# A selective scan on one core: products, scans and B's broadcast share four PSUM banks, and each group's product moves ahead of the last scan before it

## The chip, the core and the metric

The kernel runs on one core of a Trainium2 chip. The metric is device time in microseconds, the median of several executions. Engines are named as in the profile: PE (matmuls, with PEld for its weight loads), DVE (VectorE), ACT (ScalarE), POOL (GpSimd) and SP, which only issues DMAs here. Each engine runs its own list of instructions in order; engines meet at semaphores.

## The reference, cut to what matters

The input is x, 16 samples of 64 x 64 positions x 96 channels. Layer 0 normalises x, resamples it, runs a small two-layer network and adds the result to x. Layer 1 normalises again and runs a Mamba block over the 4096 positions of each sample. Its core, per channel d (192 of them) and state n (16 of them), is

```python
dA  = exp(delta[..., None] * A)
dBu = delta[..., None] * Bm[:, :, None, :] * xc[..., None]
def step(h, inp):                # one position after the other
    dA_t, dBu_t, C_t = inp
    h = dA_t * h + dBu_t
    y = einsum('bdn,bn->bd', h, C_t)
    return (h, y)
```

and its output is gated, projected and added to the layer's input.

## The kernel before

A sample is cut into 8 chunks of T = 512 positions. In a chunk there are 192 x 16 pairs (d, n) = 24 tiles of 128 partitions x 512 positions. A tile is a unit n = 0..23; three units are a group g = 0..7 of the chunk, so a sample has 64 groups and the kernel 1024. A unit needs: on ACT the exponential `av` (L1008, eight buffers); on DVE the scan `hs` (L1140, `tensor_tensor_scan`, six buffers), which reads `av` from SBUF and its row of products from PSUM; on POOL the product with C, `hc` (L1181, six buffers), and after the group's third unit a copy of the last column, `state` (L1185). PE sums over n into `py` (L855, function `reduce`), after the group's three `hc`.

The products themselves are made once per group. PE spreads B's row over the partitions into the PSUM bank `pb` (L846, `spread_b`, one bf16 matmul), and DVE multiplies `rep_u` (delta times x, from SBUF) by `pb` into the three banks of `b3` (L1134, one instruction of 128 x 1536). In the order of DVE's list a group is: product, scan 0, scan 1, scan 2. The product waits for the broadcast (`pe_b`) and for the scan before it (`dve_h`, since it overwrites what that scan reads); scan 0 waits for the product (`dve_bu`) and for the `state` of two groups before (`pool_st`); each scan waits for its `av`. PE's broadcast for group g waits until the product of group g-1 is done, and stands in PE's list after unit 3g-2, before the `reduce` of group g-2 (after unit 3g-1).

PE, ACT and DVE have a second stream of work between the units: layer 0 of the samples ahead and the projections of the chunks ahead. Its steps are rows (position, step) of a plan, where a position is a unit of the sample, 0 to 191. PE works a row off after the unit of its position; ACT evicts it 4 units later (`LAG`), DVE does its part 3 units later. The results take turns in three PSUM banks `cb`, each freed by its eviction. The plan's function `level` spreads PE's steps by assumed costs, and `warm` fills the lightly loaded groups with dummy matmuls (L710). The steps that matter below, all in groups 32 to 35 of a sample: `DG` at position 98 makes a bias, and DVE adds a constant to it into `cst` (L1123) after unit 101; `D_lo`, `D_hi` from position 100 on (PE L794, L798), whose evictions on ACT (L965) wait for `cst`; `WG` at 102, evicted by DVE into `b1a` (L1120), for which the first `W_f` (PE L769) waits; `X` at 104 and 106 (PE L810), evicted by ACT with a silu (L982). From there to about group 29 of the next sample the second stream is dense. The plan of the last sample but one has less of it, and that of the last has only the projections and the output step `OUT` (PE L837, L838). One product of the stream, the padding step at the end of a plan, is evicted by DVE (L1100).

Of the kernel before, what the change touches and what calls it, by code (L numbers as in the profile page):

```python
# [9 lines left out]
ALU = mybir.AluOpType  # L10
ACT = mybir.ActivationFunctionType

NS, HH, WW, C = 16, 64, 64, 96
# [8 lines left out]
T = 512  # L22
NC8 = L // T
NJ, NQ = DI // 32, DSTATE // 4
NU = NJ * NQ
NG = NU // 3
NHC, NAV, NHS = 6, 8, 6
# [170 lines left out]
def build(nc, A):  # L198
    ctx = ExitStack()
    with ctx:  # L200
        def sb(name, shape, dt=F32):
            return ctx.enter_context(nc.sbuf_tensor(name, shape, dt))

        def ps(name, shape):
            return ctx.enter_context(nc.psum_tensor(name, shape, F32))
# [37 lines left out]
        selb = sb("selb", [C, NQ, 128], BF16)  # L243
# [39 lines left out]
        bc3 = sb("bc3", [C, 4, T], BF16)  # L283
        rep_d = sb("rep_d", [128, 2, NJ, T])
        rep_u = sb("rep_u", [128, 2, NJ, T])
        cs = sb("cs", [128, 2, NQ, T])
        av = sb("av", [128, NAV, T])
        hs = sb("hs", [128, NHS, T])
# [10 lines left out]
        yv = sb("yv", [C, T])  # L299

        cb = ps("cb", [128, RING, 512])
        b3 = ps("b3", [128, 3, 512])
        pb = ps("pb", [128, 512])
        py = ps("py", [128, 512])

        ld_s = sem("ld_s")
# [36 lines left out]
        ru_ld = [sem("ru_ld0"), sem("ru_ld1")]  # L343
        cs_ld = [sem("cs_ld0"), sem("cs_ld1")]
        pe_b = sem("pe_b")
        act_a = sem("act_a")
        dve_bu = sem("dve_bu")
        dve_h = sem("dve_h")
# [8 lines left out]

        xtok = A["x"].rearrange("s h w c -> s (h w) c")
        otok = A["out"].rearrange("s h w c -> s (h w) c")

        def rows_of(m):

# [120 lines left out]
        def count(sm, v):  # L483

            return max(v, 0)
# [8 lines left out]
        def _(sp):  # L494
# [136 lines left out]
            def c_part(st, k, n):  # L631
                G = st.s * NC8 + k
                at = AT["sp"]
                if not ((G < -1 or G + 1 >= NS * NC8)):

                    p = (k + 1) % 2
                    if n == at["du"]:
                        sp.wait_ge(pool_u, count(pool_u, G + 2))
                        sp.sem_inc(sp_passed, 1)
                        sp.dma_start(du_d[p].rearrange("(t p) f -> p t f", p=C), dlt[:, :, :]).then_inc(du_st, 16)  # L640
                    if n == at["rd"][0]:
                        sp.wait_ge(dl_st, count(dl_st, (G + 2) * 16))
                        sp.sem_inc(sp_passed, 1)
                        sp.wait_ge(act_a, count(act_a, G * NU))
                        sp.sem_inc(sp_passed, 1)
# [43 lines left out]
        def _(pe):  # L689
# [151 lines left out]
            def spread_b(G, k, g):  # L841

                if g == 0:
                    pe.wait_ge(pool_bc, count(pool_bc, G * 2 + 2))
                pe.wait_ge(dve_bu, count(dve_bu, G * NG + g))
                pe.matmul(pb[:, :], selb[:, g % NQ, :], bc3[:, k % 4, :], start=True, stop=True).then_inc(pe_b, 1)  # L846

            def reduce(s, k, g):
                G = s * NC8 + k
# [205 lines left out]
        @block.vector  # L1055
        def _(dve):
            dve.memset(wx[:, :, :], 0.0).then_inc(zset, 1)
            dve.memset(bc3[:, :, :], 0.0).then_inc(zset, 1)
            dve.memset(mhalf[:, :], -0.5)
            dve.memset(eps[:, :], 1e-5)  # L1060
            dve.memset(zero_state[:, :], 0.0)
            dve.memset(zero2[:, :], 0.0).then_inc(zset, 1)
            dve.wait_ge(ld_w, count(ld_w, 16 * len(loads)))
            n_set = [0]

            def setup(ins):
                n_set[0] += 1
                ins.then_inc(setup_v, 1)
                dve.wait_ge(setup_v, count(setup_v, n_set[0]))

            for f in range(NF):
                setup(dve.tensor_scalar(g2[:, 1, f, 0:C], w2t[:, f, :], coef[:, f, 1:2], None, ALU.mult))
            setup(dve.tensor_tensor(fcst[:, :], b1t[:, :], coef[:, :, 1], ALU.mult))
            setup(dve.tensor_tensor(fcst[:, :], fcst[:, :], coef[:, :, 0], ALU.add))
            for f in range(NF):
                setup(dve.tensor_scalar(w2c[:, f, :], w2t[:, f, :], coef[:, f, 2:3], None, ALU.mult))

            for tap in range(3):
                setup(dve.tensor_tensor(wtap[:, tap, :, :], winx.rearrange("c (t p) -> c t p", t=2),
                                        cwb.rearrange("c (p t k) -> c k t p", t=2, k=3)[:, tap], ALU.mult))  # L1080

            def finish():
                dve.wait_ge(setup_a, count(setup_a, 2))
                setup(dve.tensor_scalar(nega[:, :, :], nega[:, :, :], -1.0, None, ALU.mult))
                dve.wait_ge(pe_conv, count(pe_conv, N_FIRST + 3))
                dve.tensor_copy(wlin[:, :], cb[0:C, 0, 0:C]).then_inc(cb_free[0], 1)
                dve.tensor_tensor(cbase[:, :], cb[0:C, 1, 0:1], b2t[:, :], ALU.add).then_inc(cb_free[1], 1)
                dve.tensor_copy(spare[:, 2:3], cb[0:C, 2, 0:1]).then_inc(cb_free[2], 1)
                assert n_set[0] == N_SETUP

            def step(st, key):
                name, b = key[:2]
                if name in ("SLD", "WLD", "DLD", "DW", "WARM", "SG1", "SG2", "DG1", "DG2") or name in BATCHED or name == "OUT":
                    return
                i = st.at[key]
                bank = cb[:, i % RING]
                fr = cb_free[i % RING]
                if name == "PAD":
                    dve.wait_ge(pe_conv, st.done(i))
                    dve.tensor_copy(spare[:, i % RING:i % RING + 1], bank[0:C, 0:1]).then_inc(fr, 1)  # L1100
                    return
                x = st.sample(key)
                if name == "ST":
                    dve.wait_ge(fr, st.freed(i))
                    dve.bn_stats(bst[:, 0, b, :], xs_of(b)).then_inc(xs_bn, 1)
                    if b == 7:
                        dve.wait_ge(xs_bn, count(xs_bn, x * 8 + 8))
                        dve.wait_ge(act_v[0], count(act_v[0], x))
                        dve.bn_aggr(mv[:, 0, :], bst[:, 0].rearrange("c a b -> c (a b)")).then_inc(dve_m[0], 1)
                elif name == "D_hi":  # L1110
                    for bank_free, n_free in st.freed_all([i, st.find(("D_lo", b), key)]):
                        dve.wait_ge(bank_free, n_free)
                    dve.bn_stats(bst[:, 1, b, :], x1s[:, b % 2, :]).then_inc(x1_bn, 1)
                    if b == 7:
                        dve.wait_ge(x1_bn, count(x1_bn, x * 8 + 8))
                        dve.wait_ge(act_v[1], count(act_v[1], x))
                        dve.bn_aggr(mv[:, 1, :], bst[:, 1].rearrange("c a b -> c (a b)")).then_inc(dve_m[1], 1)
                elif name == "WG":
                    dve.wait_ge(pe_conv, st.done(i))
                    dve.tensor_tensor(b1a[:, :], bank[:, 0:NF], b1t[:, :], ALU.add).then_inc(fr, 1)  # L1120
                elif name == "DG":
                    dve.wait_ge(pe_conv, st.done(i))
                    dve.tensor_tensor(cst[:, :], bank[0:C, 0:1], cbase[:, :], ALU.add).then_inc(fr, 1)  # L1123

            def unit(s, k, n):
                G = s * NC8 + k
                hf, g, q = n // 12, n // 3, n // 3 % NQ
                if n == 0:
                    dve.wait_ge(ru_ld[k % 2], count(ru_ld[k % 2], s * (4 * 64) + (k // 2 + 1) * 64))
                if n % 3 == 0:  # L1130

                    dve.wait_ge(pe_b, count(pe_b, G * NG + g + 1))
                    dve.wait_ge(dve_h, count(dve_h, G * NU + n))  # L1133
                    dve.tensor_tensor(b3[:, :, :], rep_u[:, k % 2, 3 * hf:3 * hf + 3, :],  # L1134
                                      pb[:, None, :].broadcast_to([128, 3, T]), ALU.mult).then_inc(dve_bu, 1)
                    dve.wait_ge(pool_st, count(pool_st, G * NG + g + 1 - NHS // 3))
                    dve.wait_ge(dve_bu, count(dve_bu, G * NG + g + 1))
                dve.wait_ge(act_a, count(act_a, G * NU + n + 1))  # L1138
                start = state[:, g, n % 3:n % 3 + 1] if k > 0 else zero_state[:, 0:1]
                dve.tensor_tensor_scan(hs[:, n % NHS, :], av[:, n % NAV, :], b3[:, n % 3, :], start, ALU.mult, ALU.add)\  # L1140
                    .then_inc(dve_h, 1)

            run(lambda row: row[0] + LAG["bn" if row[1][0] in ("ST", "D_hi") else "dve"], unit, step, lambda st, k, n: None, lambda st, k, n: None, finish)

        @block.gpsimd
# [158 lines left out]
```

## Time and profile before

| what | value |
|---|---|
| runs: median (lowest to highest) of 3 | 6343.9 us (6341.24 to 6345.12) |
| profiled execution, first to last instruction | 6343.7 us, 99100 instructions |
| busy: PE, DVE, ACT, POOL | 95%, 90%, 80%, 82% of the span |
| scans L1140 | 3072, mean 1263 and 1264 ns |
| products L1134 | 1024, mean 1761 ns |
| broadcasts L846 | 1024, mean 397 ns |
| first and last product start | 328.2 and 6322.1 us |

The profiled execution's own time is its span, 6343.7 us; it lies 0.2 us below the median of the runs. Busy shares are averages over the whole span; PE's matmuls are pipelined, so a busy PE is not PE at its peak. A full sample lasts about 375.6 us; the sixth one, from 2216.1 to 2591.7 us, is taken below as the example.

### The profile page before, as it was taken

What the parts mean: (1) busy time and instruction counts of PE and PEld (TensorE: products, weight loads), DVE (VectorE), ACT (ScalarE), POOL (GpSimd) and SP (SyncE); (2) the same over time, 40 slices, a digit from 0 to 9 for tenths busy, and PEclk for the clock granted to TensorE, in tenths of its full rate; (3) what the DMA queues carried; (4) which work ended last, traced back from release to release, by engine and by line L of the source; (5) the groups of instructions that cost most, each with busy time, mean ns of one, the idle gap of its engine ahead of it and who ended that gap; (6) DMA issues with size and microseconds to landing.
All of it is one profiled execution on the core that took longest, in us unless ns stands there. A gap on an engine that the chain in (4) does not pass through costs nothing. (4 is left out here: it accounts for less than half of the span.)

```text
span 6343.7 us, 99100 instructions
## 1 busy us (share of the span) xinstructions
PE 6036.5 (95%) x32260; PEld 3123.0 (49%) x32260; DVE 5685.5 (90%) x4459; ACT 5097.3 (80%) x8658; POOL 5209.8 (82%) x5092
## 2 busy tenths in 40 slices
PE   8999999999999999999999999999999999998776
PEld 5645445454554545545455544545455454554222
DVE  0089999999999999999999999999999999999998
ACT  4588888888888888888888788888888888887664
POOL 0078888888888888888888888888888888888988
PEclk9999999999999999999999999999999999998665
DMA  3367676676767667675676767667676766767553
GB/s 95 88 165 170 160 167 157 163 162 169 169 154 168 155 165 170 155 182 142 167 162 162 173 156 169 155 164 163 167 169 156 166 154 165 168 142 160 129 124 75
DMA packets 805826, 983.25 MB, mean 155 GB/s; under 512 B 391258, under 2 KB 417542, under 8 KB 805318
## 3 DMA queue, kind: packets, MB, share of 16 engines
q1 hardware_dynamic: 805318, 976.92, 65.4%
q8 instruction: 265, 4.34, 0.3%
q14 instruction: 243, 1.99, 0.1%
HBM read 717.71 MB, written 259.00 MB: 154 GB/s over the span
## 5 line engine op out<-in xcount | busy, mean ns | idle before, releaser
L1181 POOL TENSOR_TENSOR hc<-hs,cs 128x512 f32<-128x512 f32 x3072 | 3835.6, 1271 | 692.7 <-DVE hs L1140 505.6
L1140 DVE TENSOR_TENSOR_SCAN hs<-av,state,b 128x512 f32<-128x512 f32 x2688 | 3257.8, 1263 | 88.6 <-POOL state L1185 4.9
L1008 ACT ACTIVATE av<-rep_d,nega 128x512 f32<-128x512 f32 x3072 | 2096.7, 713 | 41.5 <-DVE hs L1140 36.8
L1134 DVE TENSOR_TENSOR b<-rep_u,pb 128x1536 f32<-128x1536 f32 x1024 | 1803.5, 1761 | 211.0 <-PE pb L846 124.7
L855 PE MATMUL py<-hc,rsel 128*32 128x512 f32 x6144 | 1141.6, 634 | 40.6 <-POOL hc L1181 39.7
L769 PE MATMUL cb<-xu,w1a 96*128 96x392 f32 x2400 | 984.3, 513 | 27.7 <-DVE b1a L1120 17.4
L774 PEld LDWEIGHTS cb<-w2c,g 128*98 128x98 f32 x9600 | 885.9, 167 | 169.7 <-issue 106.9
L774 PE MATMUL cb<-w2c,g 128*98 128x96 f32 x9600 | 910.7, 252 | 17.4 <-ACT g L956 9.3
L956 ACT ACTIVATE g<-cb,b1a 128x392 f32<-128x392 f32 x1200 | 679.5, 579 | 87.0 <-PE cb L769 78.8
L810 PE MATMUL cb<-xn,wtap 96*96 96x512 f32 x1536 | 723.3, 607 | 2.4 <-ACT xn L1029 2.4
L769 PEld LDWEIGHTS cb<-xu,w1a 96*128 96x128 f32 x2400 | 414.5, 191 | 415.4 <-issue 199.3
L846 PE MATMUL pb<-bc,selb 96*128 96x512 bf16 x1024 | 406.6, 397 | 140.5 <-DVE b L1134 140.4
L1140 DVE TENSOR_TENSOR_SCAN hs<-av,zero_state,b 128x512 f32<-128x512 f32 x384 | 466.9, 1264 | 11.8
L949 ACT ACTIVATE vr<-cb 98x384 f32<-98x384 f32 x400 | 194.9, 487 | 320.2 <-PE cb L774 318.2
L810 PEld LDWEIGHTS cb<-xn,wtap 96*96 96x96 f32 x1536 | 243.5, 166 | 400.4 <-issue 380.0
L855 PEld LDWEIGHTS py<-hc,rsel 128*32 128x32 f32 x6144 | 157.2, 110 | 455.7 <-POOL hc L1181 225.0
L1218 POOL TENSOR_TENSOR dlt<-dlt,xcs 96x1024 f32<-96x1024 f32 x128 | 301.8, 2358 | 68.5 <-DMA delta_scratch<-dlt 68.5
L846 PEld LDWEIGHTS pb<-bc,selb 96*128 96x128 bf16 x1024 | 103.7, 101 | 508.1 <-issue 246.3
L763 PE MATMUL cb<-up_h,t1r 128*96 128x196 f32 x1600 | 345.7, 339 | 7.7 <-DMA t1r<-t_scratch 7.5
L837 PE MATMUL cb<-wo,xcs 96*128 96x96 f32 x2048 | 341.0, 292 | 3.7 <-POOL xcs L1233 3.5
L1233 POOL TENSOR_TENSOR xcs<-xcs,zs 96x512 f32<-96x512 f32 x256 | 324.1, 1266 | 20.1
L837 PEld LDWEIGHTS cb<-wo,xcs 96*128 96x128 f32 x2048 | 291.5, 205 | 86.0 <-issue 49.5
(109 smaller groups left out, 6703.4 us busy)
## 6 DMA issues: line engine op xcount, KB each, us to landing
rep_d<-delta_scratch SPq DMA_DIRECT2D x512, 384.0 KB, 7.0
rep_u<-deltax_scratch SPq DMA_DIRECT2D x512, 384.0 KB, 6.3
cs<-c_scratch SPq DMA_DIRECT2D x512, 256.0 KB, 5.9
delta_scratch<-dlt SPq DMA_DIRECT2D x128, 384.0 KB, 3.1
deltax_scratch<-dlt SPq DMA_DIRECT2D x128, 384.0 KB, 9.2
t1r<-t_scratch SPq DMA_DIRECT2D x160, 240.0 KB, 6.5
v_scratch<-v2s SPq DMA_DIRECT2D x192, 192.0 KB
xb<-in_x SPq DMA_DIRECT2D x128, 192.0 KB, 4.6
```

The costliest lines, as they stand in the source:

```text
L763: mm = pe.matmul(bank[0:C, e * 2 * GH:(e + 1) * 2 * GH], t1r[:, m % 2, i2 % 5, :], up_h[:, :], start=True, stop=True)
L769: mm = pe.matmul(bank[:, 0:BC], w1a[:, 128 * f:128 * f + 128], xu[:, b % 2, :], start=True, stop=True)
L774: mm = pe.matmul(bank[0:GH, C * j:C * j + C], g2[:, b % 2, f, GH * j:GH * j + GH], w2c[:, f, :], start=(f == 0), stop=(f == NF - 1))
L810: mm = pe.matmul(bank[0:C, :], wtap[:, tap, t, :], xn[:, k2 % 2, tap:tap + T], start=(tap == 0), stop=(tap == 2))
L837: pe.matmul(o, xcs[:, p, t, tb], wo[:, t, :], start=(t == 0), stop=False)
L846: pe.matmul(pb[:, :], selb[:, g % NQ, :], bc3[:, k % 4, :], start=True, stop=True).then_inc(pe_b, 1)
L855: mm = pe.matmul(py[32 * j:32 * j + 32, :], rsel[:, :], hc[:, (3 * g + j) % NHC, :], start=(q == 0), stop=(q == NQ - 1), skip_group_check= ...
L956: act.activation(g2[:, b % 2, f, :], bank[:, 0:BC], ACT.Square, bias=b1a[:, f:f + 1]).then_inc(fr, 1)
L1008: act.activation(av[:, n % NAV, :], rep_d[:, k % 2, j, :], ACT.Exp, scale=nega[:, q, j:j + 1])\
L1134: dve.tensor_tensor(b3[:, :, :], rep_u[:, k % 2, 3 * hf:3 * hf + 3, :], pb[:, None, :].broadcast_to([128, 3, T]), ALU.mult).then_inc(dve_b ...
L1140: dve.tensor_tensor_scan(hs[:, n % NHS, :], av[:, n % NAV, :], b3[:, n % 3, :], start, ALU.mult, ALU.add)\
L1181: pool.tensor_tensor(hc[:, n % NHC, :], hs[:, n % NHS, :], cs[:, k % 2, g % NQ, :], ALU.mult)\
```

## The change

The banks `b3` and `pb` become one tensor of four banks, `b4`. Group by group the three product banks are 2, 1, 0 (even groups, walked backwards) or 1, 2, 3 (odd groups), and the broadcast is put into the bank of the group's third product, 0 or 3; the product instruction overwrites it in place. The two banks of the first two products of a group are those that the group before has already scanned, so the product needs only that group's first two scans. In DVE's list the order becomes: scan 0, scan 1, product of the next group, scan 2. PE's broadcast for group g waits for the scans of group g-2 in place of the product of group g-1, as its bank is that of group g-2's third product.

```diff
-        b3 = ps("b3", [128, 3, 512])
-        pb = ps("pb", [128, 512])
+        b4 = ps("b4", [128, 4, 512])
...
+        def banks(g):
+            return b4[:, 2::-1, :] if g % 2 == 0 else b4[:, 1:4, :]
+        def bank_of(g, e):
+            return 2 - e if g % 2 == 0 else 1 + e
...
-                pe.wait_ge(dve_bu, count(dve_bu, G * NG + g))
-                pe.matmul(pb[:, :], selb[:, g % NQ, :], bc3[:, k % 4, :], start=True, stop=True).then_inc(pe_b, 1)
+                pe.wait_ge(dve_h, count(dve_h, (G * NG + g - 1) * 3))
+                pe.matmul(b4[:, bank_of(g, 2), :], selb[:, g % NQ, :], bc3[:, k % 4, :], start=True, stop=True)\
+                    .then_inc(pe_b, 1)
...
+            def times_b(G, g):
+                k = G % NC8
+                if g == 0:
+                    dve.wait_ge(ru_ld[k % 2], count(ru_ld[k % 2], G // NC8 * (4 * 64) + (k // 2 + 1) * 64))
+                dve.wait_ge(pe_b, count(pe_b, G * NG + g + 1))
+                dve.wait_ge(dve_h, count(dve_h, (G * NG + g) * 3 - 1))
+                out, hf = banks(g), g // NQ
+                b = b4[:, bank_of(g, 2), :]
+                dve.tensor_tensor(out, rep_u[:, k % 2, 3 * hf:3 * hf + 3, :], b[:, None, :].broadcast_to([128, 3, T]), ALU.mult)\
+                    .then_inc(dve_bu, 1)
+
             def unit(s, k, n):
...
+                if G == 0 and n == 0:
+                    times_b(0, 0)
                 if n % 3 == 0:
-
-                    dve.wait_ge(pe_b, count(pe_b, G * NG + g + 1))
-                    dve.wait_ge(dve_h, count(dve_h, G * NU + n))
-                    dve.tensor_tensor(b3[:, :, :], rep_u[:, k % 2, 3 * hf:3 * hf + 3, :],
-                                      pb[:, None, :].broadcast_to([128, 3, T]), ALU.mult).then_inc(dve_bu, 1)
                     dve.wait_ge(pool_st, count(pool_st, G * NG + g + 1 - NHS // 3))
                     dve.wait_ge(dve_bu, count(dve_bu, G * NG + g + 1))
+                if n % 3 == 2 and not (G + 1 == NS * NC8 and g + 1 == NG):
+                    times_b(G + (g + 1) // NG, (g + 1) % NG)
                 dve.wait_ge(act_a, count(act_a, G * NU + n + 1))
```

The wait for `rep_u` at a chunk's first product moves with the product. Nothing else in the plan, the lags or the other engines' lists is changed.

## Rows read from the trace of the kernel before

**Rows 1.** Windows view: the sixth sample and the last two; columns named at the top.

```profile
core 0: us, PE busy (x) PEld busy (x) DVE busy (x) ACT busy (x) POOL busy (x), PEclk, DMA share, GB/s
...
2216.10:2591.70 375.60, 368.81 (x2024) 192.05 (x2021) 354.71 (x278) 317.15 (x542) 325.61 (x319) 1.00 0.69 163
...
5606.00:5970.30 364.30, 311.12 (x1457) 145.65 (x1451) 349.50 (x268) 273.00 (x442) 323.04 (x316) 0.85 0.64 145
5970.30:6322.10 351.80, 247.87 (x769) 79.21 (x764) 339.27 (x253) 214.68 (x322) 312.20 (x305) 0.63 0.49 111
```

**Rows 2.** Waits of DVE over five full samples: total us, times, longest.

```profile
DVE b L1134 <- PE pb L846: 37.7, 56, 1.3
```

**Rows 3.** Waits of PE in the sixth sample that DVE or POOL ended.

```profile
PE cb L769 <- DVE b1a L1120: 1.3, 1, 1.3
PE py L855 <- POOL hc L1181: 1.1, 3, 0.4
PE cb L794 <- DVE cst L1123: 0.8, 1, 0.8
PE pb L846 <- DVE b L1134: 0.7, 2, 0.4
```

**Rows 4.** Timeline of DVE, groups 26 to 35: start us, us, work, [idle before].

```profile
2368.83 1.76 DVE L1134 TENSOR_TENSOR b<-rep_u,pb 128x1536 f32<-128x1536 f32 x1 [0.99 <-PE pb L846]
...
2386.81 1.76 DVE L1134 TENSOR_TENSOR b<-rep_u,pb 128x1536 f32<-128x1536 f32 x1
2388.66 3.62 DVE L1140 TENSOR_TENSOR_SCAN hs<-av,state,b 128x512 f32<-128x512 f32 x3
2392.39 1.76 DVE L1134 TENSOR_TENSOR b<-rep_u,pb 128x1536 f32<-128x1536 f32 x1
...
2411.01 3.63 DVE L1140 TENSOR_TENSOR_SCAN hs<-av,state,b 128x512 f32<-128x512 f32 x3
2414.56 0.12 DVE L1123 TENSOR_TENSOR cst<-cb,cbase 96x1 f32<-96x1 f32 x1
...
2423.38 0.66 DVE L1113 BATCH_NORM_STATS2 bst<-x1s 96x6 f32<-96x512 f32 x1
2423.96 0.14 DVE L1120 TENSOR_TENSOR b1a<-cb,b1t 128x3 f32<-128x3 f32 x1
```

**Rows 5.** Timeline of PE in the same stretch.

```profile
2368.41 0.38 PE L846 MATMUL pb<-bc,selb 96*128 96x512 bf16 x1
...
2386.08 0.38 PE L846 MATMUL pb<-bc,selb 96*128 96x512 bf16 x1
...
2414.74 0.67 PE L794 MATMUL cb<-xt,wtot 96*96 96x256 f32 x2 [0.77 <-DVE cst L1123]
...
2425.17 2.82 PE L810 MATMUL cb<-xn,wtap 96*96 96x512 f32 x6
```

**Rows 6.** Timeline of ACT in the same stretch.

```profile
2409.26 1.32 ACT L1008 ACTIVATE av<-rep_d,nega 128x512 f32<-128x512 f32 x2
2414.77 0.47 ACT L965 ACTIVATE x1s<-cb,cst 96x256 f32<-96x256 f32 x1 [4.18 <-issue]
...
2424.43 0.68 ACT L982 ACTIVATE xcs<-cb,tapb 96x512 f32<-96x512 f32 x1
```

**Rows 7.** Timeline of POOL in the same stretch.

```profile
2390.09 3.73 POOL L1181 TENSOR_TENSOR hc<-hs,cs 128x512 f32<-128x512 f32 x3 [1.73 <-DVE hs L1140]
...
2409.14 3.71 POOL L1181 TENSOR_TENSOR hc<-hs,cs 128x512 f32<-128x512 f32 x3
```

**Rows 8.** Timeline of PE in the last sample, around one output step.

```profile
6005.64 0.61 PE L846 MATMUL pb<-bc,selb 96*128 96x512 bf16 x1 [2.05 <-DVE b L1134]
6006.18 1.93 PE L855 MATMUL py<-hc,rsel 128*32 128x512 f32 x6
...
6013.27 0.63 PE L846 MATMUL pb<-bc,selb 96*128 96x512 bf16 x1
```

**Rows 9.** Timeline of DVE at the same place.

```profile
6003.82 1.76 DVE L1134 TENSOR_TENSOR b<-rep_u,pb 128x1536 f32<-128x1536 f32 x1
```

**Rows 10.** Windows view of the same place; columns as in the first group.

```profile
6003.00:6026.00 23.00, 15.56 (x54) 6.31 (x52) 22.19 (x17) 15.84 (x25) 22.61 (x22) 0.50 0.50 123
```

More of the change, by code:

```diff
@@ L1123, in step @@
                     dve.tensor_tensor(cst[:, :], bank[0:C, 0:1], cbase[:, :], ALU.add).then_inc(fr, 1)
+            def times_b(G, g):
[8 more added lines that the diff above has]
+                    .then_inc(dve_bu, 1)
             def unit(s, k, n):
[L1126 to L1129, printed above, removed]
+                G, g = s * NC8 + k, n // 3
+                if G == 0 and n == 0:
+                    times_b(0, 0)
                 if n % 3 == 0:
-                    dve.wait_ge(pe_b, count(pe_b, G * NG + g + 1))
-                    dve.wait_ge(dve_h, count(dve_h, G * NU + n))
-                    dve.tensor_tensor(b3[:, :, :], rep_u[:, k % 2, 3 * hf:3 * hf + 3, :],
-                                      pb[:, None, :].broadcast_to([128, 3, T]), ALU.mult).then_inc(dve_bu, 1)
                     dve.wait_ge(pool_st, count(pool_st, G * NG + g + 1 - NHS // 3))
                     dve.wait_ge(dve_bu, count(dve_bu, G * NG + g + 1))
+                if n % 3 == 2 and not (G + 1 == NS * NC8 and g + 1 == NG):
+                    times_b(G + (g + 1) // NG, (g + 1) % NG)
                 dve.wait_ge(act_a, count(act_a, G * NU + n + 1))
                 start = state[:, g, n % 3:n % 3 + 1] if k > 0 else zero_state[:, 0:1]
-                dve.tensor_tensor_scan(hs[:, n % NHS, :], av[:, n % NAV, :], b3[:, n % 3, :], start, ALU.mult, ALU.add)\
-                    .then_inc(dve_h, 1)
+                dve.tensor_tensor_scan(hs[:, n % NHS, :], av[:, n % NAV, :], b4[:, bank_of(g, n % 3), :], start,
+                                       ALU.mult, ALU.add).then_inc(dve_h, 1)
             run(lambda row: row[0] + LAG["bn" if row[1][0] in ("ST", "D_hi") else "dve"], unit, step, lambda st, k, n: None, lambda st, k, n: None, finish)
```

## Prediction

> **What bounds the kernel now.** I read the windows by sample first. Fourteen of the sixteen samples carry the dense second stream; one lasts 375.6 us, and PE is busy in 368.8 and DVE in 354.7 of them [rows 1]. Shares so close together do not say which engine leads, so the next view is who waits for whom. DVE waits for PE's broadcast 37.7 us in five samples, 7.5 us a sample [rows 2]. PE waits for DVE or POOL only 1.3 + 1.1 + 0.8 + 0.7 = 3.9 us a sample [rows 3]; 0.7 of that, two of 64 broadcasts, is the wait that the change loosens. The reader should see the asymmetry: most of the time PE goes at its own pace (with ACT, which empties its banks) and DVE follows.
>
> The timeline shows where. At 2368.83 the product begins 0.04 us after its broadcast (2368.41 + 0.38), having waited 0.99 us: PE leads there [rows 4, 5]. At 2386.81 the product of group 29 starts without a wait, 0.35 us after its broadcast (2386.08 + 0.38), and from there to 2414.74 DVE runs without one. At 2414.74 PE waits 0.77 us for `cst`, and ACT, which had nothing to issue past that eviction, stood still for 4.18 us [rows 5, 6]. So DVE's chain sets the pace in one short stretch of a sample, groups 29 to 35, and PE with ACT in the rest. In the last sample PE's granted clock is 0.63 on average and its busy time 247.9 of 351.8 us [rows 1]: there DVE leads.
>
> **The change, part by part.** *DVE's cycle.* Now a product takes 1.76, scan 0 follows 0.09 after its end, three scans take 3.62, and the next product starts 0.11 later (2388.66 + 3.62 to 2392.39): 5.58 us a group [rows 4]. The two gaps are waits for DVE's own results. Where no such wait stands, an instruction starts before its predecessor is recorded as ended: the statistics at 2423.38 end at 2424.04, the next instruction starts at 2423.96, 0.08 earlier [rows 4]. Three scans in 3.62 with two such overlaps make one scan 1.26. In the new order only the product waits for the scan just before it. Product to scan 2 is 1.76 - 0.08 = 1.68, scan 2 to scan 0 and scan 0 to scan 1 are 1.18 each, scan 1 takes 1.26, then the gap of 0.11: 5.41, so 0.17 less. Bounds: 0, if a scan does not overlap the product ahead of it, to 0.20 if all three junctions and the gap come out a little better. I take 0.17, the row's own overlap.
>
> A rule of the Trainium skill speaks against that saving. "VectorE: DVE Perf Modes", section "The DRAIN you can't avoid", states that the next DVE instruction does not start until the pipeline of the last has emptied, and that taking semaphores away saves nothing. The 0.08 overlap above disagrees with it. By the rule the cycle stays at 5.58; the time is then that of rival C.
>
> *In place, and the reversed banks.* No row has DVE reading and writing one PSUM bank. In-place cost bounds: nothing below; above, if reading and writing that third of the product took turns, 512 of 1536 columns twice, 1.76 / 3 = 0.59 us a group. I take nothing: the four-bank form moves as many elements, and one engine goes over them in one order. The backward walk over banks has the same bounds.
>
> *PE's broadcast.* Its release moves from the end of product g-1 to the end of group g-2's third scan. Counted from the start of product g-1, that was 1.76 + 0.06 (6003.82 to 6005.64 [rows 8, 9]) and becomes 1.68 + 1.26 + 0.06 = 3.0, since that scan now follows the product. Product g starts 5.41 after product g-1, so with 0.38 for the matmul 2.0 us of slack remain, before 3.4. Instructions behind it on PE (a `reduce`, then steps) are held with it only where PE is early.
>
> *DVE's place relative to PE.* This is the price. Where a product is released by its broadcast, the group's scans used to follow at once. Now scan 2 of the group before comes first: relative to the same broadcast everything DVE does comes later, scans 0 and 1 by 1.0 us (1.68 + 1.18 against 1.85), and what stands behind a third scan by far more, as the next group's product is put ahead of it. `cst` is such a step: it stands after unit 101, the third scan of group 33, and so now also behind the product of group 34.
>
> *The stretch from group 29, walked through.* The broadcast of group 29 ends at 2386.46 either way (2386.08 + 0.38), as PE leads up to it. DVE, one scan later relative to PE, now just waits for it: product at 2386.50 instead of 2386.81. Five cycles of 5.41 and 0.03 for the chunk's boundary put the product of group 34 at 2413.58 (now 2414.74). Its scan 2, of group 33, starts 1.68 later at 2415.26, and `cst` 1.18 after that at 2416.44, ending 2416.56. Now it ends at 2414.68 [rows 4]. It comes 1.9 us later.
>
> ACT then starts its queue at 2416.65 instead of 2414.77. From there it works without a pause to the silu of the first `X`, 2424.43 to 2425.11, and PE's second `X` at 2425.17 waits for just that bank [rows 5, 6]. It moves to 2427.1. POOL does not change this: its `hc` of group 29 waits for DVE [rows 7], its last one ends about 2.4 us later than now, and POOL is then busy without a gap to 2412.85, which becomes 2415.2; PE's `reduce` of group 32 then ends at about 2416.1, ahead of `cst`. `b1a` comes 0.6 later by the same count, at 2424.7, and is hidden by the 2427.1. From here PE leads again, now 1.9 us late, and DVE's shorter cycle only makes it wait longer: 11 us a sample (64 x 0.17).
>
> *Other edges*, at nothing: the `rep_u` wait moves one scan up, but by the code its loads are issued after units 7 to 13 of the chunk before, which leaves more than three groups; `pool_st` has a cycle of 5.4 us, and DVE has slack where POOL is late. If those covers were gone, DVE would wait at a chunk's first product or first scan.
>
> **The sum.** Fourteen stretches x 1.9 = +26.6 us. The last two samples: 128 cycles x 0.17 = -21.8. Against it, at a granted clock of 0.50, the 1.2 GHz level (PE was idle for a third of this sample), the broadcast after an output step comes late: it was 7.63 us after the one before it (6005.64 to 6013.27 [rows 8, 10]). From the product at 6003.82 the count is now 2.94 to the third scan's end, 1.45 until POOL's `hc` lets the `reduce` start (a third of 3.73 for the multiply [rows 7], and the waits), 7.09 from it to the broadcast and 0.63 for it: 12.1, while the product could start after two cycles, 10.85. That is 1.3 us in each of about ten chunks, +13. For some five other places in the sample before the last where the broadcast is already close, I add one scan each, 1.2 us, an estimate: +6. Together -3. The forecast is 6343.7 + 26.6 - 3 = 6367 us; the span is 0.2 below the median of the runs, so the same number stands for the median: 0.37% slower.
>
> **Rivals.** *A, faster.* DVE leads everywhere, and each group saves 0.17: 1024 x 0.17 = 174, 6170 us. For it: the chain of waits ends in DVE's rows, and DVE's cycle repeats at 5.58. Against it: 7.5 us a sample of waiting for broadcasts. A milder form is bounded by PE's own waits, 3.9 us a sample: if `cst` came no later than now, the loosened broadcast let PE run ahead and ACT did not bind, 14 x 3.9 = 55 less, 6289. It decides at `cst`: before 2414.7 on the clock above, faster; after, slower. Chance 0.16 for both, mostly values a little under 6331.
>
> *B, no change.* The second eviction of `D` and ACT's queue catch up: ACT stood still for 4.18 us there with its exponentials several units ahead of DVE, and if the wait of `X` had room of 1.9 us that the row does not show, the +26.6 falls away and -3 is left: 6341. Chance 0.20.
>
> *C, slower by more.* No saving in the cycle: then `cst` ends at 2386.50 + 5 x 5.58 + 0.03 + 1.85 + 1.18 + 0.13 = 2417.7, 3.0 late, +42, and the last two samples lose about 10 (ten chunks x 0.95 and little else): 6396. Or the product in place costs up to 0.59: DVE's own time, 368 a sample (375.6 - 7.5), grows by 64 x (0.59 - 0.17) = 27 to 395, 16 x 19 = +310, 6654. From +0.3 us a product it passes PE's pace. Chance 0.08 for both.
>
> **How the numbers follow.** The forecast has 0.56. Within 0.2%, about 13 us and what a measurement of this kernel can tell from no change, lies B. Slower holds the forecast and C, 0.64; faster A, 0.16; same 0.20. The likeliest case alone, with the saving between 0.20 and 0.10, ranges from 6358 to 6380. The range takes in B and the first half of C and leaves A's far end and the in-place price out: 6328 to 6394.
>
> **What would show it.** Right: products of about 1.76 us and unwaited cycles of 5.41; DVE's waits for broadcasts grown from 7.5 to some 20 us a sample; a sample of 377.5 us; ACT's idle time before L965 grown from 4.2 to about 6 us, and PE's wait for `cst` from 0.8 to over 2. Wrong: a sample shorter than 375 us, products longer than 1.8 us, cycles still at 5.58, or PE waiting for broadcasts.

## The result and the profile after

The changed kernel takes 6435.0 us against 6342.8 us (medians of four runs each); the ratio of the means is 1.0142, 95% interval 1.0128 to 1.0157. The forecast was 6367 us, slower by 0.37%; the sign was right and the loss is four times as large, outside the range. The profiled execution's span is 6436.1 us, 92.4 more than before. The page's costliest groups that the change touches, the product with C and the product with B on the page of before and then all three after:

```profile
L1181 POOL TENSOR_TENSOR hc<-hs,cs 128x512 f32<-128x512 f32 x3072 | 3835.6, 1271 | 692.7 <-DVE hs L1140 505.6
L1134 DVE TENSOR_TENSOR b<-rep_u,pb 128x1536 f32<-128x1536 f32 x1024 | 1803.5, 1761 | 211.0 <-PE pb L846 124.7
```
```profile
L1197 POOL TENSOR_TENSOR hc<-hs,cs 128x512 f32<-128x512 f32 x3072 | 3855.1, 1273 | 814.6 <-DVE hs L1156 766.7
L1156 DVE TENSOR_TENSOR_SCAN hs<-av,state,b 128x512 f32<-128x512 f32 x2688 | 3255.4, 1261 | 0.4 <-POOL state L1201 0.4
L1142 DVE TENSOR_TENSOR b<-rep_u,b 128x1536 f32<-128x1536 f32 x1024 | 1804.3, 1762 | 533.3 <-PE b L853 480.5
```

Product and scans last what they did. What grew is waiting: DVE's for the broadcast (124.7 to 480.5 us), POOL's for the scans (505.6 to 766.7 us). The windows view of the sixth sample and the last two, with the columns of [rows 1]:

```profile
2244.10:2626.20 382.10, 372.36 (x2023) 192.66 (x2022) 348.46 (x278) 317.44 (x542) 326.01 (x319) 0.99 0.68 161
5682.40:6053.70 371.30, 320.32 (x1461) 151.42 (x1462) 343.48 (x267) 272.81 (x443) 325.49 (x319) 0.83 0.63 143
6053.70:6412.30 358.60, 253.83 (x763) 79.88 (x763) 333.23 (x253) 215.93 (x323) 311.73 (x303) 0.62 0.48 109
```

The sixth sample is 6.5 us longer. DVE is busy 6.3 us less in it; PE is busy 3.6 us *more*, with the same matmuls to do, and the granted clock is 0.99 instead of 1.00. Of the 92.4 us, the fourteen full samples have 78.1 (5355.9 instead of 5277.8 us from the first product of the first to that of the fifteenth sample) and the last two 14.8, counted to the last scan's end; the start and the end of the kernel make up the rest.

DVE's waits over five samples, beside [rows 2], and PE's in the sixth sample, beside [rows 3] (us in total, times, longest):

```profile
DVE b L1142 <- PE b L853: 155.8, 183, 4.6
```
```profile
PE py L863 <- POOL hc L1197: 3.2, 3, 2.8
PE cb L801 <- DVE cst L1131: 1.4, 1, 1.4
PE cb L817 <- ACT xcs L990: 1.2, 1, 1.2
```

PE no longer waits for a broadcast's release or for `b1a`; it waits once for 2.8 us on POOL, once on `cst`, and once on ACT. The timeline of PE shows all three, with two rows that make the difference:

```profile
2431.08 0.39 PE L853 MATMUL b<-bc,selb 96*128 96x512 bf16 x1
2434.28 0.63 PE L863 MATMUL py<-hc,rsel 128*32 128x512 f32 x3 [2.81 <-POOL hc L1197]
...
2434.96 4.44 PE L717 MATMUL py<-selb 96*32 96x512 bf16 x12
2439.33 0.39 PE L853 MATMUL b<-bc,selb 96*128 96x512 bf16 x1
...
2448.19 0.67 PE L801 MATMUL cb<-xt,wtot 96*96 96x256 f32 x2 [1.40 <-DVE cst L1131]
...
2458.62 4.51 PE L817 MATMUL cb<-xn,wtap 96*96 96x512 f32 x6 [1.21 <-ACT xcs L990]
```

The broadcasts are those of groups 32 and 33, with `reduce` of group 30 between them. The same place before, in rows not shown so far:

```profile
2400.81 0.39 PE L846 MATMUL pb<-bc,selb 96*128 96x512 bf16 x1
2401.61 0.63 PE L855 MATMUL py<-hc,rsel 128*32 128x512 f32 x3 [0.41 <-POOL hc L1181]
...
2402.28 2.75 PE L710 MATMUL py<-selb 96*32 96x512 bf16 x12
2405.40 0.39 PE L846 MATMUL pb<-bc,selb 96*128 96x512 bf16 x1 [0.37 <-DVE b L1134]
```

From broadcast to broadcast it took 4.59 us and takes 8.25. The wait is 2.4 longer; it stands at 2.80 or 2.81 us in all fourteen full samples. Then the twelve filler matmuls on `selb`, which fill PE's spare time and whose result nothing uses, last 4.44 instead of 2.75, and the six of `X` 4.51 instead of 2.82 [rows 5]: 1.7 us in each place, behind a wait of PE. The windows view gives the granted clock of the first wait and the stretch behind it, and of the wait at `X` and the stretch behind that:

```profile
2431.00:2434.30 3.30, 0.49 (x6) 0.12 (x5) 3.17 (x3) 2.52 (x7) 3.22 (x4) 1.00 0.00 0
2436.90:2439.40 2.50, 2.50 (x8) 0.76 (x7) 1.38 (x2) 0.30 (x1) 2.42 (x3) 0.62 0.86 235
2457.40:2458.60 1.20, 0.01 (x1) 0.00 (x0) 1.10 (x2) 1.19 (x3) 1.20 (x2) 1.00 0.89 189
2460.80:2463.10 2.30, 2.30 (x7) 0.51 (x6) 2.00 (x2) 0.00 (x0) 1.46 (x3) 0.59 0.28 53
```

In this sample the granted clock is full during the wait and falls behind it, to 0.62 and 0.59 over these stretches, most of each at the 1.2 GHz level, so PE pays a second time. In eight of the fourteen full samples it falls before the wait at `reduce` ends: in the second sample the stretch from 902.80 to 904.20, the end of the wait, is at 0.50, and the twelve fillers take 4.78 us. Now DVE, ACT and POOL in this stretch, beside [rows 4, 6, 7]:

```profile
2416.79 1.76 DVE L1142 TENSOR_TENSOR b<-rep_u,b 128x1536 f32<-128x1536 f32 x1
...
2422.18 1.76 DVE L1142 TENSOR_TENSOR b<-rep_u,b 128x1536 f32<-128x1536 f32 x1
2423.85 3.62 DVE L1156 TENSOR_TENSOR_SCAN hs<-av,state,b 128x512 f32<-128x512 f32 x3
2427.57 1.76 DVE L1142 TENSOR_TENSOR b<-rep_u,b 128x1536 f32<-128x1536 f32 x1
...
2439.76 1.76 DVE L1142 TENSOR_TENSOR b<-rep_u,b 128x1536 f32<-128x1536 f32 x1 [1.47 <-PE b L853]
...
2448.01 0.13 DVE L1131 TENSOR_TENSOR cst<-cb,cbase 96x1 f32<-96x1 f32 x1
...
2467.38 1.76 DVE L1142 TENSOR_TENSOR b<-rep_u,b 128x1536 f32<-128x1536 f32 x1 [4.58 <-PE b L853]
```
```profile
2448.22 0.47 ACT L973 ACTIVATE x1s<-cb,cst 96x256 f32<-96x256 f32 x1 [3.92 <-issue]
...
2457.89 0.68 ACT L990 ACTIVATE xcs<-cb,tapb 96x512 f32<-96x512 f32 x1
```
```profile
2421.18 2.51 POOL L1197 TENSOR_TENSOR hc<-hs,cs 128x512 f32<-128x512 f32 x2
2425.21 1.27 POOL L1197 TENSOR_TENSOR hc<-hs,cs 128x512 f32<-128x512 f32 x1 [1.52 <-DVE hs L1156]
...
2426.57 1.27 POOL L1246 TENSOR_TENSOR xcs<-xcs,yv 96x512 f32<-96x512 f32 x1
...
2431.73 2.49 POOL L1197 TENSOR_TENSOR hc<-hs,cs 128x512 f32<-128x512 f32 x2
```

An unwaited cycle is 2427.57 - 2422.18 = 5.39 us. POOL takes the first two `hc` of group 29, then stands still 1.52 us for the third scan, which now follows a product. From 2425.21 it has work without a gap to 2434.22, the end of `hc` of group 30, for which `reduce` waits. Counted from the product of group 29, the third `hc` starts 8.42 us on; before, 2390.09 and two thirds of 3.73 less 2386.81 [rows 4, 7] make it 5.8. The 2.6 us go through POOL's queue almost whole into PE's wait, which is 2.4 longer.

### The profile page after: what moved, and what is told of

The parts are those of the page before. It is cut to its first block, busy times and chain, and to the rows that moved or that the text cites. A ratio compares the mean times of both kernels' runs of the same rounds, so it can differ in the third digit from the quotient of the medians.

```text
span 6436.1 us, 99100 instructions
## 1 busy us (share of the span) xinstructions
PE 6098.4 (95%) x32260; PEld 3138.8 (49%) x32260; DVE 5584.7 (87%) x4459; ACT 5099.9 (79%) x8658; POOL 5214.4 (81%) x5092
## 4 chain that ended last, share of the span: by engine, by line
PE 62%; DVE 12%; POOL 10%; ACT 9%; issue 5%; DMA 2%; SPq 0%; DVEq 0%; POOLq 0%; ACTq 0%
PE cb L781 10%; PE py L863 10%; PE cb L776 9%; PE cb L817 8%; POOL hc L1197 7%; DVE hs L1156 7%; DVE b L1142 5%; PE cb L823 3%; PE cb L770 3%; ACT av L1016 3%; PE cb L827 3%; PE cb L805 2%; PE cb L844 2%; PE b L853 2%; PE cb L787 2%
## 5 line engine op out<-in xcount | busy, mean ns | idle before, releaser
L1197 POOL TENSOR_TENSOR hc<-hs,cs 128x512 f32<-128x512 f32 x3072 | 3855.1, 1273 | 814.6 <-DVE hs L1156 766.7
L1142 DVE TENSOR_TENSOR b<-rep_u,b 128x1536 f32<-128x1536 f32 x1024 | 1804.3, 1762 | 533.3 <-PE b L853 480.5
L817 PE MATMUL cb<-xn,wtap 96*96 96x512 f32 x1536 | 751.5, 627 | 22.4 <-ACT xcs L990 15.7
L853 PE MATMUL b<-bc,selb 96*128 96x512 bf16 x1024 | 408.1, 399 | 74.6 <-DVE hs L1156 73.5
L1249 POOL TENSOR_TENSOR xcs<-xcs,zs 96x512 f32<-96x512 f32 x256 | 325.4, 1271 | 20.1
```

The source lines that it names most:

```text
L817: mm = pe.matmul(bank[0:C, :], wtap[:, tap, t, :], xn[:, k2 % 2, tap:tap + T], start=(tap == 0), stop=(tap == 2))
L853: pe.matmul(b4[:, bank_of(g, 2), :], selb[:, g % NQ, :], bc3[:, k % 4, :], start=True, stop=True)\
L1142: dve.tensor_tensor(out, rep_u[:, k % 2, 3 * hf:3 * hf + 3, :], b[:, None, :].broadcast_to([128, 3, T]), ALU.mult)\
L1197: pool.tensor_tensor(hc[:, n % NHC, :], hs[:, n % NHS, :], cs[:, k % 2, g % NQ, :], ALU.mult)\
```

## The experiments

Two theories. **H**: PE's in-order list is held by `reduce`, because POOL's last `hc` of a group now comes a product later, and the broadcast behind it is held too; `cst` comes late on top, and each long wait of PE is paid again in clock. **C**, the forecast's: `cst` alone is late. A rival to both, **B**: the shared banks or the product in place cost the time. All runs in one table; the ratio is that of the means, to executions of the kernel before taken beside each run. "Full" is the fourteen full samples and "last two" the rest to the last scan, both in us from one profiled execution, less the 5277.8 and 721.5 us of before. A fall of the clock more or less is worth 2 to 3 us there, and the profiled execution can lie off the median of its runs: e9's is 9.4 us below it (6355.1), e10's 6.5 below, e6's 6.3 above (6308.1), e1's 4.8 above, the others within 3. So differences of a few us are not read:

| run | median us | ratio to before (95%) | full | last two |
|---|---|---|---|---|
| the change | 6435.0 | 1.0142 (1.0128 to 1.0157) | +78.1 | +14.8 |
| e1_old_order | 6338.1 | 0.9996 (0.9988 to 1.0005) | +20.1 | -20.1 |
| e6_old_place | 6301.8 | 0.9938 (0.9926 to 0.9951) | -17.6 | -20.3 |
| e7_old_place_wait | 6345.6 | 1.0004 (0.9995 to 1.0013) | -0.7 | +1.1 |
| e3_old_order_28_35 | 6383.5 | 1.0066 (1.0052 to 1.0079) | +32.4 | +5.0 |
| e12_new_order_28_35 | 6382.0 | 1.0061 (1.0048 to 1.0075) | +53.3 | -16.7 |
| e4_no_dummies_96 | 6414.4 | 1.0116 (1.0102 to 1.0130) | +60.5 | +8.2 |
| e10_dummies_first | 6420.2 | 1.0124 (1.0110 to 1.0137) | +59.9 | +9.4 |
| e11_dummies_first_cst | 6391.6 | 1.0078 (1.0064 to 1.0092) | +38.1 | +10.8 |
| e5_cst_early | 6388.4 | 1.0069 (1.0054 to 1.0085) | +32.4 | +12.1 |
| e8_pool_y_earlier | 6421.4 | 1.0126 (1.0113 to 1.0140) | +52.5 | +23.2 |
| e9_cst_and_pool_y | 6364.5 | 1.0032 (1.0021 to 1.0042) | -3.7 | +13.9 |
| e13_old_place_cst_pool_y | 6307.6 | 0.9946 (0.9933 to 0.9960) | -29.6 | -8.2 |

**The order undone, the banks kept.** e1 moves the product behind the third scan.

```diff
-if n % 3 == 2 and not (last group): times_b(next group)
 dve.tensor_tensor_scan(hs[:, n % NHS, :], ...)
+if n % 3 == 2 and not (last group): times_b(next group)
```

> Only the order is undone: each product stands behind the third scan again, still without a wait for that scan; the four banks in place, the reversed banks and the broadcast's release stay. Theory H (PE's reduce is held for hc, because each third scan stands behind a product, and the broadcast behind that reduce is held with it): the held reduce of group 30 is back to some 0.4 us of waiting, a full sample lasts 375 us or less, unwaited cycles stay near 5.39 us, total 6290 to 6345. Theory C (the forecast's: cst alone comes late): the same total. Theory B (PE and DVE sharing banks, or the product in place, costs the time): the loss stays, 6400 to 6440.

B falls: the loss goes with the order. But the full samples stay 20 us above before. In this edit the product still stood ahead of `cst`, which the list puts behind unit 101; PE waited some 1.54 us for it in each full sample, and its granted clock fell within 2.4 us behind that in ten of the fourteen. e6 mends that: the product stands at the head of the next unit, where it was. The edit against the changed kernel, shortened:

```diff
 if n % 3 == 0:
+    times_b(G, g)
     dve.wait_ge(pool_st, ...)
...
-if n % 3 == 2 and not (last group): times_b(next group)
```

> As the first run (order undone, four banks and product in place kept, the product does not wait for the scan just before it), but the product stands where it stood before the change, behind the steps that follow a third scan; in the first run it had come to stand ahead of cst. cst then comes some 1.6 us sooner than there. Theory H: full samples at or under the 375.6 us of before, the last two samples as in the first run (8 and 12 us less than before): total 6300 to 6325. Rival: PE's waits gather in one place, TensorE's clock falls behind it as in the first run, and full samples stay at 377 us: total 6335 to 6345.

It came out so, 6301.8, and beats both kernels. The timeline of DVE shows `cst` back behind the third scan of its group:

```profile
2411.32 3.62 DVE L1153 TENSOR_TENSOR_SCAN hs<-av,state,b 128x512 f32<-128x512 f32 x3
2414.86 0.13 DVE L1131 TENSOR_TENSOR cst<-cb,cbase 96x1 f32<-96x1 f32 x1
2414.91 1.75 DVE L1142 TENSOR_TENSOR b<-rep_u,b 128x1536 f32<-128x1536 f32 x1
```

The four banks are what makes this possible: the next product writes none of the banks that the third scan reads, so it need not wait for it, and the cycle is 5.37 us in the old order. e7 puts that wait back (`dve_h` at `(G * NG + g) * 3`, without the `- 1`).

> As the run above, and the product waits for the third scan ahead of it, as before the change: only the banks, the product in place and the broadcast's earlier release are left of the change. Cycle 5.58 us. If the shorter cycle is what the last two samples gain from, they are back at 364 and 357 us and the total is that of before, 6335 to 6345; if the broadcast's earlier release is, they stay short and the total is 6315 to 6330. Theory B: over 6360.

The cycle is 5.58 and everything is as before, the last two samples too. So banks, place and earlier release of the broadcast are worth nothing by themselves, and the shorter cycle in the old order is worth 44 us (6345.6 to 6301.8).

**Where in a sample.** e3 has the old order around groups 28 to 35 only (as in e1, ahead of `cst`). e12 is the reverse: it is e6 except for these groups, where the product stands between the second and the third scan. Its edit against the changed kernel, shortened:

```diff
+if n % 3 == 0 and not 28 <= (m - 1) % 64 <= 35:  # m = k * NG + g
+    times_b(G, g)
...
-if n % 3 == 2 and not (last group):
+if n % 3 == 2 and 28 <= m <= 35:
     times_b(next group)
```

> The new order everywhere except around groups 28 to 35 of each sample, where the product stands behind the third scan. Theory H and theory C: the loss of the full samples (6.5 us each) sits in these groups, so a full sample is back near 375.6 us; what the last two samples lost stays for the most part (some 10 to 15 us): total 6345 to 6365. Theory B: the loss stays, 6420 to 6440. A third possibility, that the late scans only move the stall to the next place with little room: 6380 to 6420.

> The order undone as in the run at 6302 us, except that for groups 28 to 35 of each sample the product stands between the second and third scan. Theory H: these eight groups of 64 carry the whole loss of the full samples, some 5.5 to 8 us each, and the last two samples keep nearly all that the shorter cycle gave: total 6380 to 6415. If the loss is spread over a sample: 6305 to 6335.

e3 came out where its third possibility had it, but it has e1's fault at `cst`, so it does not decide. e12 does: eight groups of 64 in the new order cost 53.3 + 17.6 = 71 us over e6, of the 78.1 + 17.6 = 96 that the new order costs in the full samples when it stands everywhere. Its `reduce` of group 30 waits 2.77 us again.

**Mending PE's side.** e4 leaves out the 15 filler matmuls between `reduce(30)` and the broadcast of group 33 (rows at 96 of the plan); e10 puts them ahead of that `reduce`; e11 is e10 with `cst` earlier. The edit of e10:

```diff
-out += [(p, ("WARM", p, i)) ...
+out += [(p - 2 * (p == 96), ("WARM", p, i)) ...
```

> The new order, and the 15 matmuls into the spare rows of py that stand between reduce(30) and the broadcast of group 33 are left out (they compute nothing that is used). Theory H: the broadcast of group 33 comes some 4 us sooner after reduce(30), DVE and with it cst about 1.5 us sooner, and a sample loses some 2 to 4 us less: total 6375 to 6405. Theory C: the dummies stand ahead of cst's place with room, nothing changes: 6425 to 6440.

> The new order, and the 15 matmuls into spare rows of py (same number, same operands) stand ahead of reduce(30) instead of between it and the broadcast of group 33. PE is then busy while POOL's hc is late. Theory H with the clock (the idle time costs twice, once as a wait and once as a lower granted clock behind it): reduce(30) waits under 0.5 us, the clock does not fall there, the broadcast of group 33 comes some 3 to 4.5 us sooner; cst stays late, so a full sample is near 379 to 381: total 6395 to 6425. If POOL's chain alone sets the loss, it moves to the next reduce as in the run without these matmuls: 6410 to 6435.

> The same, and cst one unit earlier on DVE. Theory H: both losses of the full samples go, 375.5 to 377 us each, without a change on POOL: total 6350 to 6375. If POOL's lateness has to be mended, 6380 to 6395.

H as I had put it, with the held broadcast carrying much of the loss, missed in e4 and e11; e11's 6391.6 lies where POOL's lateness has to be mended. e10's 6420.2 lies where both its ranges do. In e4 the broadcast of group 33 follows that of group 32 after 4.92 us too, and 60.5 of the 78.1 us stay. The timeline of PE in e10 shows why: `reduce(30)` waits no more and the broadcast of group 33 follows that of group 32 after 4.92 us, but the next `reduce` is held instead, and the clock falls there:

```profile
2420.54 0.39 PE L853 MATMUL b<-bc,selb 96*128 96x512 bf16 x1
2420.86 3.19 PE L717 MATMUL py<-selb 96*32 96x512 bf16 x14
...
2425.46 0.39 PE L853 MATMUL b<-bc,selb 96*128 96x512 bf16 x1 [0.66 <-DVE hs L1156]
...
2428.91 1.93 PE L863 MATMUL py<-hc,rsel 128*32 128x512 f32 x6 [2.23 <-POOL hc L1197]
```

So the fillers are only where the wait shows, and the broadcast held behind them accounts for no more than 18 of the 78 us (e4 and e10). POOL's queue is what is late.

**Mending `cst` or POOL.** e5 puts `cst` one unit earlier on DVE, ahead of the product; e8 puts POOL's two products for `y` ahead of the third `hc` for which it waits; e9 does both.

```diff
-row[0] + LAG["bn" if ... else "dve"]
+row[0] + LAG["bn" if ... else "dve"] - (row[1][0] == "DG")
```
```diff
-"pool": dict(u=23, bc=(18, 22), y=(17, 8)),
+"pool": dict(u=23, bc=(18, 22), y=(16, 7)),
```

> The new order, and cst stands one unit earlier on DVE, ahead of the product of group 34 and of the third scan of group 33. cst comes 2.9 us sooner. Theory C: ACT's queue and the second X come back to where they were, the full samples lose nothing: 14 x 6.5 = 91 less, total 6345 to 6360. Theory H: reduce(30) still waits 2.8 us and the broadcast of group 33 is still some 4 us late; only the second part goes, the wait at the second X with the fall of the clock behind it, some 2 to 3 us a sample: total 6390 to 6410.

> The new order, and POOL's two products for y (2.5 us) stand one unit earlier, ahead of the hc of a third scan, for which POOL now waits 1.5 us at group 29. Theory H: hc(30) ends some 1.5 us sooner, reduce(30) waits 1.3 instead of 2.8 us, the broadcast of group 33 comes 1.5 to 3 us sooner: total 6385 to 6420. Theory C: POOL does not bind, 6425 to 6440.

> The new order with both edits: cst one unit earlier on DVE and POOL's two products for y one unit earlier. Theory H: of the 6.5 us of a full sample some 0 to 1.5 stay, and the last two samples keep their loss: total 6350 to 6375. If the two losses are one and the same: 6385 to 6395, as with cst alone.

C falls with e5, 2 us below H's range: 32.4 us of the 78.1 stay, and `reduce(30)` still waits 2.80. e8's total ended 1 us above its range, with another 8 us lost in the last two samples; in the full ones it does what H says. Its timeline of PE, and the granted clock behind `cst` in the windows view:

```profile
2423.21 0.39 PE L853 MATMUL b<-bc,selb 96*128 96x512 bf16 x1
2423.83 0.63 PE L863 MATMUL py<-hc,rsel 128*32 128x512 f32 x3 [0.23 <-POOL hc L1197]
...
2427.20 0.39 PE L853 MATMUL b<-bc,selb 96*128 96x512 bf16 x1
...
2437.96 0.67 PE L801 MATMUL cb<-xt,wtot 96*96 96x256 f32 x2 [1.78 <-DVE cst L1131]
```
```profile
2438.50:2444.90 6.40, 6.40 (x26) 2.90 (x24) 3.51 (x4) 6.39 (x13) 6.23 (x6) 0.53 0.79 196
```

The stall at `reduce(30)` is gone, 3.99 us lie between the broadcasts, and what is left is mainly `cst` with a fall of the clock; the mend is not free either, as `reduce(29)` now waits 1.20 us for the `hc` that the products for `y` hold up. With both edits the full samples lose nothing in the profiled execution (e9, -3.7). By the profiled executions POOL's lateness is worth 32.4 + 3.7 = 36 us alone and `cst` 52.5 + 3.7 = 56; together they cost 78.1 + 3.7 = 82, as some of one hides behind the other. But e9's profiled execution lies low, as said above. If the distance of each profiled execution from its median is put on its full samples, an estimate, e9 keeps some 6 us, and the three prices are 25, 48 and 70. Either way both are real and `cst` is the larger.

**Both mends on the old order.**

> The order undone as in the run at 6302 us, with cst one unit earlier on DVE and POOL's products for y one unit earlier. In that run PE waits nowhere above 0.8 us around group 33, so there is little left for either edit: 6285 to 6305. If POOL's earlier products hold up its hc where the third scan comes early: 6305 to 6325.

It came out in the second range, though only by the last two samples, which lose 12 us to e6; the full ones gain 12, of which 6 may be e6's profiled execution. So 6307.6 is not better than e6. No run had the earlier `y` in the full samples alone.

## Why the forecast was off

*DVE's cycle*: right. 5.41 us forecast, 5.39 measured; a scan starts 1.67 us after the start of a product that lasts 1.76, and e6 against e7 gives what a dropped wait is worth in the old order, 44 us. I had set the Trainium skill's section "The DRAIN you can't avoid" ("VectorE: DVE Perf Modes") against the row as if it left no exception. That section of the Trainium skill has one, a next instruction that is not held. The section "Two Vector instructions with no wait between them" of the same page of the Trainium skill gives a model of which are held; by it, instructions whose operands all start in the same group of 32 partitions, as those of the products and scans here do, are not. The trace agrees with that: 1.67 us from start to start behind a product of 1.76. What the forecast took from the first section of the Trainium skill, that taking semaphores away saves nothing, does not hold for these 44 us, and the measurement decides.

*In place and the reversed banks*, at nothing: right. 1762 ns a product, and e7 is within 0.2% of before.

*The broadcast's release*: in full samples right, PE no longer waits for it. What A hoped for from it did not come: e7 keeps the earlier release and gains nothing.

*DVE's place relative to PE and `cst`*: the mechanism was right and the term mis-sized. Counted from the broadcast of group 32, `cst` came at 13.75 us and comes at 16.93, so 3.2 late and not 1.9. The walk had five cycles without a wait; in the trace the product of group 33 waits 1.47 us for its broadcast. In e8, where it is not held, `cst` is 2.1 late, counted from the broadcast of group 31 (18.62 before, 20.70 there). Two signs that were named did not show. ACT stood still 3.92 us before its eviction, not about 6, and PE waited 1.40 us for `cst`, not over 2, because both came there late themselves: counted from the broadcast of group 32, ACT ended its exponentials 3.4 us later than before and PE came to `cst` 2.5 later. DVE's waits for broadcasts grew to 31 us a sample, not some 20. The path from `cst` through ACT to the second `X` was as walked, 10.6 us now (2448.01 to 2458.62) and before (2414.56 to 2425.17). But the +26.6 (14 x 1.9) has to be 46 to 56 (e5 against the change, e9 against e8, by the profiled executions; 45 to 48 with the medians): the sum had the lateness too small and left out the lower clock behind the wait, 1.7 us at `X`.

*POOL*: this step failed. "POOL does not change this", the text says: its last `hc` of group 29 ends about 2.4 later and it is then busy without a gap, but "PE's `reduce` of group 32 then ends at about 2416.1, ahead of `cst`". The 2.4 was right (2.6 measured). I followed it to the `reduce` nearest to `cst` and past that of group 30, which in PE's list stands ahead of the broadcast of group 33, with the fillers between. It was already waiting 0.41 us before, one of the three waits on `hc` in [rows 3]; there was no room at all. That is the missing term, 26 us (e8 against the change) to 36 (e9 against e5) by the profiled executions, 21 to 25 with the medians; part of it again by the clock: 1.7 us behind 2.4 more of waiting. The remark that instructions behind the broadcast are held only where PE is early looked at what stands behind the broadcast, not at what stands ahead of it.

*The last two samples*: -3 forecast, +14.8 measured. The cycle's gain was sized right: e6 has -20.3, the forecast -21.8. The output step was nearly so: 1.48 us of DVE's waiting against 1.3 forecast. What I left out is a chain at `X`. The same place of the last sample in PE's timeline before, then PE's and DVE's after:

```profile
6161.99 0.61 PE L846 MATMUL pb<-bc,selb 96*128 96x512 bf16 x1 [1.77 <-DVE b L1134]
6164.39 4.78 PE L810 MATMUL cb<-xn,wtap 96*96 96x512 f32 x6
```
```profile
6251.70 0.61 PE L853 MATMUL b<-bc,selb 96*128 96x512 bf16 x1 [0.66 <-DVE hs L1156]
6253.05 1.93 PE L863 MATMUL py<-hc,rsel 128*32 128x512 f32 x6 [0.74 <-POOL hc L1197]
6254.90 5.44 PE L817 MATMUL cb<-xn,wtap 96*96 96x512 f32 x6
6260.13 0.63 PE L853 MATMUL b<-bc,selb 96*128 96x512 bf16 x1
```
```profile
6260.80 1.76 DVE L1142 TENSOR_TENSOR b<-rep_u,b 128x1536 f32<-128x1536 f32 x1 [1.42 <-PE b L853]
...
6267.00 1.76 DVE L1142 TENSOR_TENSOR b<-rep_u,b 128x1536 f32<-128x1536 f32 x1 [0.91 <-PE b L853]
...
6284.55 1.76 DVE L1142 TENSOR_TENSOR b<-rep_u,b 128x1536 f32<-128x1536 f32 x1 [1.48 <-PE b L853]
```

These are the broadcasts of groups 35 and 36. The first waits for a third scan and starts 3.0 us behind the product of group 34 instead of 1.8, as forecast. The `reduce` behind it, which did not wait before, now waits 0.74 us for the `hc` of another; the six of `X` take 5.44 instead of 4.78, at a granted clock of 0.50 instead of 0.58. From broadcast to broadcast it was 7.01 us (6161.99 to 6169.00) and is 8.43. DVE did not wait here before. Now it waits 3.8 us in these eight groups, output step included, and saves 8 x 0.19 = 1.5. That the third scan's place is the cause here is shown by e6 and e12 (-20.3 and -16.7 with the old order in nearly all groups); the two places were not undone one by one.

Of the rivals, A's condition (`cst` no later than now) is what e6 makes true, and it is faster, by 41 us; by e7 that gain is the shorter cycle's. C's prices did not arise; its sum for the end of `cst` adds up to 2417.6 and not 2417.7, which makes 2.9 us and +41.

## What to carry to other kernels

When an instruction moves behind another on an in-order engine, follow its lateness through every queue that it feeds to each instruction that stands ahead of the next link of the loop, not only to the one already known to be tight; a wait of 0.4 us in the trace says that there is no room. Price a wait of TensorE together with the stretch behind it, since it may run that at a lower clock, down to 0.50 here. And look for what a new buffer allows in the old order first: here the fourth bank made a wait needless, and the reordering that came with it cost all that and more.

## What the hardware showed beyond expectation

- In all fourteen waits of PE of 2.8 us the granted clock fell in the wait or within 1.5 us behind it, and the twelve matmuls behind took 4.44 to 4.87 instead of 2.75 us. Shorter waits do not sort by length: 1.34 us at `b1a` before had a fall of the clock within 2 us behind it in two of thirteen samples, and 1.21 us at `X` in twelve of thirteen samples of the changed kernel but in none of thirteen, at the same place and length, in e10. What decides it is open.
- A product over three PSUM banks in place, forwards or backwards, costs DVE what it cost from one bank into others: 1762 ns.
